# Splitting q and k straight out of the PSUM bank, and masking scores on VectorE, in a three-pass transformer kernel

## The reference

```python
# L0: causal self attention, cross attention, feed-forward (gelu)
x = x + attention(ln(x), ln(x), causal)
x = x + attention(ln(x), ctx)
x = x + gelu(ln(x) @ W_fc) @ W_mproj
# L1: masked self attention, cross attention, feed-forward (relu), norm after each
x = ln(x + self_attention(x, mask))
...
# L2: cross attention with a mask of its own for each sequence, norm after
# L3: cross attention with 16 heads of 64, norm after
p = softmax(q @ k.T / sqrt(d) + mask);  out = p @ v
```

## Time and profile before

| | before |
|---|---|
| median of 3 runs | 4791.93 us (4788.07 to 4794.76) |
| profiled execution, its own time | 4792.18 us |
| its span, first to last instruction | 4790.4 us |
| mean granted TensorE clock | 0.986 |
| busy: PE, DVE, ACT, POOL | 94%, 81%, 49%, 29% |

### The profile page before, as it was taken

The page is one execution under the profiler, slowest core; times in us unless marked ns, Lnnn a source line. Parts: engine busy times, 40 slices in busy tenths (PEclk is TensorE's granted clock), DMA queues, the critical chain, the costliest instruction groups (busy, mean ns, idle before and its releaser), DMA issues. The chain is left out here.

```text
span 4790.4 us, 97864 instructions
## 1 busy us (share of the span) xinstructions
PE 4512.8 (94%) x34560; PEld 3551.8 (74%) x34624; DVE 3884.1 (81%) x11141; ACT 2368.0 (49%) x6433; POOL 1381.1 (29%) x1813
## 2 busy tenths in 40 slices
PE   5999999999998899999999999979999999999998
PEld 4777777777777677777777777767777777777776
DVE  4888888888888788888888888857787787878786
ACT  2555555555454444444434343435555555555555
POOL 3333333333333133333323232321212121211212
PEclk8999999999999999999999999989999999999999
DMA  5444444444444444444444444321222212121221
GB/s 156 133 138 128 135 126 140 120 147 119 146 120 141 124 121 139 121 136 131 141 127 131 129 125 134 114 83 57 72 57 62 66 57 71 52 77 52 68 61 32
DMA packets 393272, 513.31 MB, mean 107 GB/s; under 512 B 109136, under 2 KB 360784, under 8 KB 371280
## 3 DMA queue, kind: packets, MB, share of 16 engines
q1 hardware_dynamic: 385392, 496.82, 35.5%
q10 hardware_dynamic: 7392, 10.24, 0.7%
HBM read 266.30 MB, written 236.72 MB: 105 GB/s over the span
## 5 line engine op out<-in xcount | busy, mean ns | idle before, releaser
L760 ACT ACTIVATE probs_own<-bank 128x384 f32<-128x384 f32 (+2 forms) x1280 | 598.2, 582 | 282.7 <-remote 156.5
L594 POOL TENSOR_SCALAR veps<-meanvar 128x2 f32<-128x2 f32 x256 | 63.1, 247 | 1503.3 <-DVE meanvar L899 1501.8
L1146 PE MATMUL bank<-ht,w_ff 128*128 128x256 f32 x2048 | 490.9, 383 | 0.8 <-issue 0.8
L1146 PE MATMUL bank<-w_ff,ffh 128*128 128x256 f32 x2048 | 491.1, 383 | 0.0
L1146 PE MATMUL bank<-qstack_own,kstack_own 99*128 99x256 bf16 (+2 forms) x2560 | 395.1, 265 | 31.9 <-DMA qstack_own<-nm_t_own 26.3
L1146 PEld LDWEIGHTS bank<-w_ff,ffh 128*128 128x128 f32 x2048 | 377.8, 192 | 46.8
L1146 PEld LDWEIGHTS bank<-ht,w_ff 128*128 128x128 f32 x2048 | 376.8, 191 | 46.9 <-issue 1.9
L1002 DVE CUSTOM_DVE_ANT_0 bank<-bank,mask_rows 128x256 f32<-128x256 f32 x1024 | 393.1, 474 | 2.9 <-PE bank L1146 2.9
L680 ACT ACTIVATE ht<-bank,columns_l 128x256 f32<-128x256 f32 x384 | 198.7, 578 | 382.8 <-PE bank L1208 382.6
L825 ACT ACTIVATE probs_other<-bank,negmax 128x120 f32<-128x120 f32 x1024 | 354.7, 382 | 64.4 <-DVE negmax L1126 64.2
L1146 PE MATMUL bank<-kstack_own,qstack_own 96*128 96x256 bf16 (+2 forms) x3072 | 355.4, 245 | 28.2 <-DMA qstack_own<-q_parts 19.9
(11 more groups left out here) (166 smaller groups left out, 10673.6 us busy)
## 6 DMA issues: line engine op xcount, KB each, us to landing
qstack_own<-q_parts SPq DMA_DIRECT2D x96, 768.0 KB, 6.2
kstack_own<-k_parts SPq DMA_DIRECT2D x64, 768.0 KB, 6.0
qstack_other<-q_parts SPq DMA_DIRECT2D x64, 768.0 KB, 6.3
q_parts<-q_parts_own SPq DMA_DIRECT2D x96, 384.0 KB, 2.6
k_parts<-k_parts_own SPq DMA_DIRECT2D x64, 384.0 KB, 2.7
q_parts<-q_parts_own SPq DMA_DIRECT2D x96, 256.0 KB, 2.2
q_parts<-other_parts SPq DMA_DIRECT2D x64, 384.0 KB, 2.8
other_words<-k_parts SPq DMA_DIRECT2D x64, 360.0 KB, 3.7
```

Of the source, the lines that this page charges most:

```text
L594: nc.gpsimd.tensor_scalar(veps[key][:, :], meanvar[key][:, :, 1], r["norms"][key]["eps"], None, ALU.add).then_inc(veps_ready.sem, 1)
L760: nc.scalar.activation(probs[key][0:rows, j % a.slots, 0:n], bank_of(u)[0:rows, 0:n], ACT.Exp, scale=a.scale).then_inc(a_done.sem, 1)
L1146: return nc.tensor.matmul(out, lhsT, rhs, start=first, stop=True, skip_group_check=True)
```

## The change

It has five parts, and new lists.

1. The split reads the bank. ACT writes `hi` as bfloat16 from the bank with the bias (`split_hi_`); DVE computes the rest from the bank, the bias and `hi` (two instructions of half the columns with a bias, one without); ACT casts the rest to `mid`; POOL computes `lo` as before. The bank stays held until DVE's instruction (`LAST_BY_DVE`).
2. l0's maxima go from "pe" to "dve": the mask matmul goes, and each head gets its custom instruction.
3. l1's second scores go from "pe" to "half": for the 8 even jobs the mask matmul goes and DVE adds `mask_less` to the scores in the bank, between PE and ACT (`mask_scores`). The 8 odd jobs stay.
4. l2's masking goes from after exp to before it: DVE adds `m_cols` in the bank (`mask_scores`), 8 jobs.
5. L2's `project_v` and L3's `project_v3` are copied by ACT (`project_v2`, `project_v3`).

A one-time preparation of masks loses some instructions, and its PE step goes. All lists are new; `START` of l1 goes from 31.9 to 32.3835, of l2 from 64.4657 to 64.8886.

```diff
-START = {"l0": 0.0, "l1": 31.9, "l2": 64.4657}
+START = {"l0": 0.0, "l1": 32.3835, "l2": 64.8886}
...
 READ_BY_ACT = ("context", "norm", "turn", "project_q", "project_k", "project_q3", "project_k3", "scores_exp", "ff_in",
-               "scores3", "turn3", "probs_v3")
+               "scores3", "turn3", "probs_v3", "project_v2", "project_v3")
+
+LAST_BY_DVE = {"project_q": "split_rest_q", "project_k": "split_rest_k"}
...
+    def on_dve(self, j):
+        return self.exp_on == "dve" or self.exp_on == "half" and j % 2 == 0
...
-            elif kind in ("project_q", "project_k"):
...
-                    nc.scalar.activation(dst[:, 0, :], src[:, 0, :], ACT.Identity, bias=bias[:, 0:1])
-                    nc.scalar.activation(dst[:, 1, :], src[:, 1, :], ACT.Identity, bias=bias[:, 1:2]).then_inc(a_done.sem, 1)
+            elif kind in ("split_hi_q", "split_hi_k"):
...
+                if bias is None:
+                    copy(hi, src).then_inc(hi_ready.sem, 1)
+                else:
+                    nc.scalar.activation(hi[:, 0, :], src[:, 0, :], ACT.Identity, bias=bias[:, 0:1])
+                    nc.scalar.activation(hi[:, 1, :], src[:, 1, :], ACT.Identity, bias=bias[:, 1:2]).then_inc(hi_ready.sem, 1)
+            elif kind in ("split_mid_q", "split_mid_k"):
...
+                copy(parts[:, 1, :].rearrange("p (f t) -> p f t", f=FT), x32).then_inc(mid_ready.sem, 1)
...
+            elif kind == "project_v2":
...
+                copy(v_aug[key][0:S2, 0, :, 0:D], bank_of(u)[0:S2, 0:C].rearrange("p (h d) -> p h d", d=D)).then_inc(a_done.sem, 1)
...
+                if w.new(masked_by_dve, ("mask_scores", key, j)):
+                    act_e.wait_ge(masked_by_dve.sem, w.value(masked_by_dve, ("mask_scores", key, j)))
...
+            elif kind == "project_v3":
...
+                copy(v3[:, 512 * j:512 * j + 512], bank_of(u)[0:S2, :]).then_inc(a_done.sem, 1)
...
-                    v.tensor_copy(hi, x32).then_inc(hi_ready.sem, 1)
...
-                    v.tensor_tensor(x32, x32, hi, ALU.subtract).then_inc(rest_ready.sem, 1)
...
-                    v.tensor_copy(mid, x32).then_inc(mid_ready.sem, 1)
+                if bias is None:
+                    ins = v.tensor_tensor(x32, src, hi, ALU.subtract)
                 else:
+                    for f in range(FT):
+                        ins = v.scalar_tensor_tensor(x32[:, f, :], src[:, f, :], bias[:, f:f + 1], hi[:, f, :], ALU.add, ALU.subtract)
...
-                v.tensor_tensor(p, p, most, ALU.min).then_inc(masked_by_dve.sem, 1)
+                    p, add = bank[:, :].rearrange("p (k t) -> p k t", k=QT), mask_less[:, :, :]
+                v.tensor_tensor(p, p, add, ALU.add).then_inc(masked_by_dve.sem, 1)
...
     r["atts"] = {"own": Att("causal", (w_own[:, 0], bq0, "0"), (w_own[:, 1], bk0, "0"), (w_own[:, 2], None, "0"), w_own[:, 3], bv0, "causal",
-                            "pe", "pool"),
+                            "dve", "pool"),
...
     own = Att("self", (w_own[:, 0], col["q_b"], "0"), (w_own[:, 1], col["k_b"], "0"), (w_own[:, 2], None, "0"), w_own[:, 3], spr["v_b"], "all",
-              "dve", "pe")
+              "dve", "half")
```

More of the change, by code:

```diff
@@ L46 @@
 PASSES = ("l0", "l1", "l2")
-START = {"l0": 0.0, "l1": 31.9, "l2": 64.4657}
+START = {"l0": 0.0, "l1": 32.3835, "l2": 64.8886}
+STAGE = {"own": 0, "0": 0, "x": 0, "c": 0, "m": 0, "other": 1, "1": 1, "ff": 2, "2": 2, "three": 2, "3": 2}
 SPREAD = {
-    "l0": {-2: (0.0, 0.9969)},
+    "l0": {},
     "l1": {},
@@ L64 @@
[L64 to L68, removed]
@@ L79 @@
[L79 to L83, removed]
@@ L240 @@
+            nm_rows.own.0/1.6525 store.x.0/3.7906
         """,
@@ L303, in __init__ @@
         name = PASSES[of]
-        later, wider = SPREAD[name].get(i, SPREAD[name].get(i - NB, (0.0, 1.0))) if kind not in ONCE else (0.0, 1.0)
+        spread = SPREAD[name].get(i, SPREAD[name].get(i - NB)) if kind not in ONCE else None
+        later, wider = spread[2 if kind == "store" else STAGE[key]] if spread else (0.0, 1.0)
         self.at = START[name] + i + later + wider * float(at)
@@ L357, in run @@
     when = {e: {(u.tag, u.element): u.at for u in steps} for e, steps in plan.items()}
-    masked = {(u.tag, u.element) for e in ("DVE", "POOL") for u in plan[e] if u.tag[0] == "mask_probs"}
+    masked = {(u.tag, u.element) for u in plan["POOL"] if u.tag[0] == "mask_probs"}
     banks = [ctx.enter_context(nc.psum_tensor(f"bank{i}", [P, 512], F32)) for i in range(8)]
@@ L366, in run @@
         _, b = min(free)
-        by = "ACT" if kind in READ_BY_ACT else "DVE"
-        read = (kind, key, j // 2) if kind == "probs_v" else u.tag
+        by = "ACT" if kind in READ_BY_ACT and kind not in LAST_BY_DVE else "DVE"
+        read = (kind, key, j // 2) if kind == "probs_v" else (LAST_BY_DVE[kind], key, 0) if kind in LAST_BY_DVE else u.tag
         holds[u.tag, u.element] = b, holder.get(b)
@@ L840, in _ @@
                      bank_of(u)[0:S2, :].rearrange("p (t f x) -> p t f x", t=QT, f=2)).then_inc(a_done.sem, 1)
+            elif kind == "project_v3":
+                if w.new(a_full, u.tag):
+                    act_e.wait_ge(a_full.sem, w.value(a_full, u.tag))
+                if first and j == r["first_of"]["project_v3"]:
+                    for x in "qk":
+                        reuse(act_e, w, u, spilled[x, "other"], [("spill_" + x, "other", i) for i in range(PARTS)], u.element - 1)
+                for tag in w.latest_first(a_full, [("probs_v3", "three", i) for i in range(2 * j, 2 * j + 2)], 1):
+                    if w.new(a_full, tag, 1):
+                        if w.twice:
+                            settle(act_e)
+                        act_e.wait_ge(a_full.sem, w.value(a_full, tag, 1))
+                copy(v3[:, 512 * j:512 * j + 512], bank_of(u)[0:S2, :]).then_inc(a_done.sem, 1)
             elif kind == "probs_v3":
@@ L1180, in _ @@
                 pe.wait_ge(setup_g, SETUP_ALL)
-            if kind == "masks":
-                pe.wait_ge(setup_v, len(make_masks[0]))
-                bank = take(u)
-                for t in range(QT):
-                    ins = nc.tensor.matmul(bank[:, t * P:(t + 1) * P], none_rows[:, t, :], ident[:, :], start=True, stop=True,
-                                           skip_group_check=True)
-                ins.then_inc(d_full.sem, 1)
-            elif kind == "context":
+            if kind == "context":
                 if w.new(c_loaded, ("load_c", "c", 0)):
```

464 lines of the change are left out of this document (223 added, 241 removed).

## The result

The changed kernel takes 4600.26 us, median of 4 runs (4596.59 to 4604.14), against 4791.87 for the one before on the same chip: a ratio of 0.9601, 95% interval 0.9584 to 0.9617. It is 4.0% faster.

A forecast was written before the change was run, and what follows sets the result against it. PE bounds l1 and is nearly full in l0 and l2, its gaps waits for DVE. Periods minus 3.4 us, times 31, minus 105, passages plus 10: span 4790.4 - 95 = 4695, with 1.8 beyond it 4697 us; range 4630 to 4795.

The forecast's parts named there:

- l2's term of the sum: l2's period: 1.1 of PE's 1.7 us wait on masks go, 0.6 stay on ACT, 49.2 to 48.1 us.
- The cause of l2's wait: l2's masks, both inputs in SBUF, some stretched beside POOL's `xb`: 0.88 us each, 0.60 in the bank.
- DVE's 45.8 us: l1: DVE's work per period after the change, 43.0 + 4.8 - 2.0, 95% busy.
- rival A: l1: VectorE bounds it, period 52.1 us, plus 2.8; kernel slower at 4821 us; chance 0.13.
- The price of the additions: l1: eight mask additions in the bank at 0.60 us a step, plus 4.8 us of DVE (4.7 to 7.1).
- the 43.0 us: l1: DVE's busy time per period before the change, 87.2%, the base to which additions and split were applied.
- B's mechanism: l0: DVE's chain sets the period, which gets 1.0 us longer, not 1.1 shorter; kernel 4762 us; chance 0.15.
- ACT's 1.8 and 2.1 us: Work added to ACT per sequence, 1.8 us in l0 and l1, 2.1 in l2, lying beside PE's work.
- The rest from the bank: Split in l0 and l1: DVE's 256-column instructions priced at 0.409 us recorded, 0.33 a step; plus 0.4 us in all.
- The passages: Between passes: later places in the lists and a shorter drain, a fifth of a period, plus 10 us (0 to 20).
- Rival D: All passes: PE's whole saving shows and half its waits go, l0 -3.1, l1 -1.8, l2 -1.7; 4597 us; chance 0.08.
- Rival C: l2: the wait moves to ACT and the period stays at 49.2 us; kernel 4731 us; chance 0.13.

## Why the prediction missed

**The step that failed is l2's term of the sum.** It took PE's 47.1 us of recorded busy time as work that stays, and asked only how much of the 1.7 us of waits would go. The floor was 45.5: the changed kernel does l2's matmuls in that time at a granted clock of 1.00. Of l2's 3.6 us, 2.1 were PE's recorded idle time, all of it gone where I gave 1.1 back, and 1.5 came out of "busy": about 1.1 us of longer records behind waits at full clock, and 0.3 us of matmuls at 1.2 GHz, behind the wait of 8 of 30 sequences. Two runs with the kernel before's lists show the same without the clock: with `xb` moved, and with the mask in the bank, the granted clock of l2 is 1.00 from 3600 to 4400, and PE is still recorded busy 46.4 us a period. The term is 2.5 us a period too small, 78 of the 97 us by which 4697 missed.

**The cause of l2's wait was right, and its end too.** Masks with two SBUF inputs were stretched beside GpSimd, and adding in the bank ended it (0.691, no tail). I then let the wait pass to ACT in part. On the old lists that did happen (0.6 us a period on ACT's `probs_own`), and l2 won 1.4 us there, close to my 1.1. It is the new order of steps that let PE run full. Which of its moves did that is open: with all parts on the old lists l2 stands at 47.5, and no list of l2 was tried step by step.

**l1: size right, reason partly wrong.** The masks are worth 1.76 us off PE, 1.74 when put back. The period fell by 1.4, as 0.3 came back where I had 0.55, but that stands in the runs as a cost of the new order and not as DVE's load. DVE's 45.8 us were too high (40.9), and rival A had no ground: DVE was at 85%, not 95%. The price of the additions held: with the eight additions gone DVE's l1 window shows 586.26 of 800 or 36.4 us a period, so they cost 4.5 (4.8 forecast). The 4.9 us lie for the most part in the 43.0 us that I took as fixed. Groups of DVE in l1, kernel before, then changed kernel (busy us, mean ns):

```profile
L911 DVE TENSOR_SCALAR xh<-xn_own,meanvar,rstd 128x256 f32<-128x256 f32 x34 | 27.5, 847 | 22.1 <-issue 22.1
L911 DVE TENSOR_SCALAR xh<-xn_other,meanvar,rstd 128x256 f32<-128x256 f32 x32 | 27.1, 885 | 0.0
L953 DVE TENSOR_TENSOR ot_raw_own<-ot_raw_own,k_parts_own 128x512 f32<-128x512 f32 x16 | 24.4, 1526 | 0.5
L1039 DVE CAST nm_parts_other<-nmf_other 128x32 bf16<-128x32 f32 x16 | 15.0, 936 | 0.0
```

```profile
L943 DVE TENSOR_SCALAR xh<-xn_own,meanvar,rstd 128x256 f32<-128x256 f32 x34 | 12.5, 412 | 23.5 <-issue 23.5
L943 DVE TENSOR_SCALAR xh<-xn_other,meanvar,rstd 128x256 f32<-128x256 f32 x34 | 12.4, 407 | 0.0
L1049 DVE CAST nm_parts_other<-nmf_other 128x32 bf16<-128x32 f32 x17 | 3.1, 181 | 0.6
```

`norm`'s four go from some 0.87 to 0.41 us, a cast of 32 columns from 0.936 to 0.181, and k's rest stood at 1.526 where q's took 0.693. These rows make 1.8, 0.8 and 0.8 of the 4.9 us. k's rest reads the bank in the changed kernel; the other two the change doesn't touch. In the kernel before GpSimd stands beside the long ones and not beside the short one. DVE, then POOL:

```profile
2034.74 1.69 DVE L911 TENSOR_SCALAR xh<-xn_other,meanvar,rstd 128x256 f32<-128x256 f32 x2
2041.34 0.69 DVE L953 TENSOR_TENSOR ot_raw_own<-ot_raw_own,q_parts_own 128x512 f32<-128x512 f32 x1
2042.93 1.53 DVE L953 TENSOR_TENSOR ot_raw_own<-ot_raw_own,k_parts_own 128x512 f32<-128x512 f32 x1
```

```profile
2034.86 1.42 POOL L639 TENSOR_TENSOR xb<-xb,vectors_l 128x512 f32<-128x512 f32 x1
2042.73 1.18 POOL L663 TENSOR_TENSOR q_parts_own<-ot_raw_own,q_parts_own 128x512 bf16<-128x512 f32 x1 [3.49 <-DVE q_parts_own L959]
```

In the changed kernel at the same point of its l1 (`norm` at 2037.45, 0.73 us for two) POOL is idle until 2038.37. So the stretch that I saw in l2's masks was in l1's 43.0 us too, and the new order took it out. No run moved GpSimd's work in l1 alone.

**l0: size right, reason wrong.** 1.1 forecast, 1.2 measured, but not from PE's masks: with those back on PE the period is the same 46. DVE's chain, and where its steps stand, set l0's pace. That is B's mechanism, though the 1.0 us that B added didn't come. The part alone in the old order costs 2.4%, and undoing a third of it in the new one wins 0.3%. What won l0's 1.2 us is the new order together with the split; the share of each stays open.

**ACT's 1.8 and 2.1 us show no cost**, as forecast: ACT stands at 65% in l2, v's copies back on DVE change nothing, and with the split alone in the old lists l0 and l1 keep their periods. **The rest from the bank** costs 0.475 us with a bias, median, where I had 0.41: 0.07 on six instructions, hidden. **The passages** cost nothing where I had plus 10 us: a list's place isn't a time. **Rival D** named 4597, but by l0 -3.1, l1 -1.8, l2 -1.7; measured are -1.2, -1.4, -3.6, so the total is met by a wrong split. **Rival C** is refuted in the new lists, PE having no wait on ACT in l2.

The deeper fault is a sum of independent prices. On the kernel before, the parts alone give -0.45% (split), +2.4% (l0's maxima) and -0.9% (l2's mask); all five parts on those lists give +4.1%; with the new lists -4.0%. l1's half of the masks and v's copies were not tried alone on them. The prediction treated the lists as neutral and priced nothing for them.

## What to carry to other kernels

An engine's recorded busy time is no floor: before calling it work that stays, look at whether the same matmul group takes longer behind a wait than elsewhere, and at the granted clock in short windows there. Do it for many periods: the sequence shown first above is one of the 8 in 30 with a low clock, and alone it would overstate what the clock costs. Price a wait of PE with what stands behind it: 2.1 us of idle time came with 1.5 us more in l2 of the kernel before, and a single wait of 2.9 us with as much again. Where each engine follows an order written by hand, moving a step's work and choosing its order are one change, and a part tried with the other's order can even have the wrong sign.

## What the runs showed of the hardware

Behind 2.90 us of waiting PE ran at a granted clock of 0.50 and took 6.8 us for matmuls that take 3.9 otherwise. Behind two waits of 1.11 and 0.56 us, in the kernel before, the granted clock fell in 8 of 30 sequences and stayed at 1.00 in 22. Eight minima with two SBUF inputs took 8.71 us beside GpSimd instructions of 512 columns, and GpSimd's own went from 1.27 to as much as 1.72 us there, so both sides pay. Eight additions with one input in a bank took 4.88 us beside the same GpSimd instructions, which stayed at 1.27 to 1.30.
